# Moving the "+1" of a gate's sigmoid from ScalarE to VectorE

## The reference

```
x0 = xf @ w1 + b1;  x1 = xf @ w2 + b2;  x2 = xf @ w3 + b3      # [b, n], n = 4096 pixels
sm = softmax(x0[:, :, None] * x1[:, None, :], axis=1)
feats = einsum('bn,bnm->bm', x2, sm)                            # [b, n]
return sigmoid(feats) * x
```

## Time and profile before

| | |
|---|---|
| median of three executions | 5820.21 us |
| the profiled execution's own time | 5822.9 us |
| its span, first to last instruction | 5821.0 us |
| PE busy | 5343.6 us (92%) |
| DVE busy | 4126.1 us (71%) |
| ACT busy | 4092.6 us (70%) |
| POOL busy | 1925.5 us (33%) |
| granted clock of TensorE, mean over the span | 0.948 of full |

### The profile page before, as it was taken

How to read it: one execution, slowest core, us unless ns; L and a number is a source line. 1 busy time by engine, 2 the same in 40 slices (tenths; PEclk the granted TensorE clock), 3 DMA queues, 4 the chain that set the end, 5 groups by cost and what they waited for, 6 DMA issues and landing times.

```text
span 5821.0 us, 111758 instructions
## 1 busy us (share of the span) xinstructions
PE 5343.6 (92%) x43240; PEld 2782.0 (48%) x43240; DVE 4126.1 (71%) x8699; ACT 4092.6 (70%) x6401; POOL 1925.5 (33%) x1588
## 2 busy tenths in 40 slices
PE   5789999999999999999999999999999989999976
PEld 2435536454453645446363554645445364544514
DVE  6647777777777777677777777777777777767715
ACT  1367768678686877868677786867768587786863
POOL 1224234242423424233342423424242342423302
PEclk8899999999999999999999999999999999999976
DMA  2000110102011020101102011010201102010000
GB/s 71 16 30 19 59 30 19 61 10 66 23 56 33 12 64 14 63 26 38 46 7 70 19 59 30 21 59 10 67 22 56 33 13 64 14 62 27 16 15 30
DMA packets 163165, 211.10 MB, mean 36 GB/s; under 512 B 13136, under 2 KB 146000, under 8 KB 162640
## 3 DMA queue, kind: packets, MB, share of 16 engines
q1 hardware_dynamic: 138064, 136.82, 7.3%
q0 software_dynamic: 24576, 67.14, 4.0%
HBM read 136.80 MB, written 67.11 MB: 35 GB/s over the span
## 4 chain that ended last, share of the span: by engine, by line
PE 68%; ACT 14%; DVE 9%; issue 5%; POOL 2%; DMA 1%; SPq 0%; ACTq 0%; DVEq 0%; POOLq 0%
PE PS L1036 33%; PE PS L1200 16%; PE PS L1191 6%; ACT n_x L478 2%; PE PS L1295 2%; PE PS L1065 2%; PE PS L1087 2%; PE PS L1134 2%; ACT big L552 1%; DVE stats L753 1%; ACT work L516 1%; ACT work L515 1%; ACT xin L478 1%; ACT attn L524 1%; ACT attn L530 1%
## 5 line engine op out<-in xcount | busy, mean ns | idle before, releaser
L552 ACT ACTIVATE big<-PS 128x1024 f32<-128x1024 f32 x1376 | 1365.9, 1024 | 482.9 <-PE PS L1191 409.6
L552 ACT ACTIVATE soft<-PS 128x1024 f32<-128x1024 f32 x672 | 676.5, 1024 | 370.3 <-PE PS L1191 356.1
L391 POOL DMA_INDIRECT quant_H<-emb_t,idx x512 | 487.4, 952 | 990.4 <-DVE idx L777 806.6
L1036 PE MATMUL PS<-e_hi,n_hi 128*128 128x512 f16 x2048 | 783.3, 382 | 21.8 <-DVE m L771 13.4
L1036 PE MATMUL PS<-e_lo,n_hi 128*128 128x512 f16 x2048 | 780.1, 381 | 0.0
L1036 PE MATMUL PS<-e_hi,n_lo 128*128 128x512 f16 x2048 | 779.7, 381 | 0.0
L1200 PE MATMUL PS<-big,w 128*4 128x512 f32 x5504 | 770.0, 649 | 2.2 <-ACT big L552 2.2
L753 DVE BATCH_NORM_STATS2 stats<-XT 128x6 f32<-128x512 f32 x1024 | 651.7, 683 | 21.1 <-POOL XT L407 11.3
L1191 PE MATMUL PS<-rhs,lhs 12*128 12x512 bf16 x4096 | 565.5, 401 | 75.5 <-ACT big L552 47.1
L777 DVE FIND_INDEX8 idx<-m,work 128x8 uint32<-128x1024 f32 x512 | 622.1, 1219 | 0.0
L771 DVE CUSTOM_DVE_ANT_0 work<-PS,e_bias,m 128x512 f32<-128x512 f32 x512 | 384.1, 750 | 220.8 <-PE PS L1036 215.4
(11 more groups left out here) (216 smaller groups left out, 11128.0 us busy)
## 6 DMA issues: line engine op xcount, KB each, us to landing
xin<-x SPq DMA_DIRECT2D x128, 512.0 KB, 3.8
out<-yout SPq DMA_DIRECT2D x128, 512.0 KB, 2.9
quant_H<-emb_t,idx POOLq DMA_INDIRECT x512, 2.7
XT<-emb SPq DMA_DIRECT2D x1, 1024.0 KB, 5.0
XT<-wh SPq DMA_DIRECT2D x1, 256.0 KB, 5.0
XT<-wqv SPq DMA_DIRECT2D x1, 256.0 KB, 5.2
XT<-wk SPq DMA_DIRECT2D x1, 128.0 KB, 5.2
w_sb<-w SPq DMA_DIRECT2D x1, 128.0 KB, 5.1
```

The source lines that it names most:

```text
L391: nc.gpsimd.indirect_dma_start(quant[:, g % 2, u, :], None, emb_t, bass.IndirectOffsetOnAxis(ap=idx[:, t % (2 * GT), 0:1], axis=0),).then_ ...
L552: nc.scalar.activation(E[h % 3][:, z * 1024:(z + 1) * 1024], bank(2 * z, 2), ACT.Exp).then_inc(exped.sem, 1)
L1036: ins = mm(dst, a, b, start=first and j == 0, stop=last and j == 2)
```

## The change

ACT's "+1" is removed, with its semaphore `gate_oned`. DVE now waits for `gate_exped` (raised by the exponential), adds 1 itself with a `tensor_scalar` of 128x32 with an immediate, SBUF to SBUF and in place, and then takes the reciprocal behind a `link`.

```diff
             def gate_exp(im):
                 act.wait_ge(*gate_arg.after(im))
                 nc.scalar.activation(gate[:, 1, :], gate[:, 0, :], ACT.Exp, scale=-1.0).then_inc(gate_exped.sem, 1)
-                act.wait_ge(*gate_exped.after(im))
-                nc.scalar.activation(gate[:, 1, :], gate[:, 1, :], copy, bias=ones[:, 0:1]).then_inc(gate_oned.sem, 1)
...
                 last.then_inc(gate_arg.sem, 1)
-                dve.wait_ge(*gate_oned.after(im))
+                dve.wait_ge(*gate_exped.after(im))
+                link(v.tensor_scalar(gate[:, 1, :], gate[:, 1, :], 1.0, None, ALU.add))
                 v.reciprocal(gate[:, 2, :], gate[:, 1, :]).then_inc(gate_made.sem, 1)
```

More of the change, by code:

```diff
@@ L249, in build @@
         filled, exped, summed = step("filled", 2 * HALVES), step("exped", 2 * HALVES, 2), step("summed", HALVES, 3)
-        acc_kept, acc_turned, gate_arg, gate_exped, gate_oned, gate_made = (
-            step(n, 1) for n in ("acc_kept", "acc_turned", "gate_arg", "gate_exped", "gate_oned", "gate_made"))
+        acc_kept, acc_turned, gate_arg, gate_exped, gate_made = (
+            step(n, 1) for n in ("acc_kept", "acc_turned", "gate_arg", "gate_exped", "gate_made"))
         g_normed, g_spread = step("g_normed"), step("g_spread")
```

## The result

The changed kernel takes 5866.5 us (median of four executions, 5862.9 to 5876.9); the kernel before took 5819.8 us beside it (5818.3 to 5822.9). The ratio is 1.0083 with a 95% interval of 1.0065 to 1.01: 46.7 us slower. The forecast was 5848 us with 5815 to 5860, so the sign is right and the size is too small: the time lies 6.5 us above the range. The profiled execution of after took 5868.4 us (span 5866.5, mean granted clock 0.942 in place of 0.948).

The account below looks back on a forecast made before the run. ACT was taken to bound the touched stretch up to 890.87, PE having some room. Six images at 0.92 us plus nine at 2.6, less 0.2, gave about +28 on 5820.2: 5848 us, range 5815 to 5860.

Parts of the forecast that it names:

- The addition by itself: On DVE, between exponential and reciprocal: the 32-element addition, undisturbed, was estimated at 0.17 us.
- Held by POOL: At DVE's addition: POOL's subtraction L401 starts first and blocks it until its end, making the reciprocal 1.82 us later.
- ACT's part: On ACT at the gate: dropping the "+1" frees 0.23 us an image, 3.7 us over sixteen.
- Queueing: From the spread to ACT's L515: PE idle time absorbs 0.90 of 1.82 us, so ACT is 0.92 us late per image.
- The clock's price: Behind PE's new idle time before the spread: matmuls at the lower clock cost 1.7 us more, making 2.6 us an image.
- Nine images out of fifteen: Behind PE's new idle time: the clock was taken to fall in nine images of fifteen, bounds none and all.
- What ACT is late there goes through rigidly to 890.87 and on: From ACT's L515 onward: ACT has no idle time to absorb its lateness, so +0.92 us per image passes on.
- Not held: Rival at DVE's addition: POOL does not block it, giving a small gain, 5816.5 us; chance 0.22.
- off the path: Rival behind the gate: the engines' room absorbs the whole 1.82 us, total effect between -3.7 and +5 us; chance 0.08.
- Held, but PE keeps its clock: Rival behind the spread: POOL blocks the addition but PE's clock never falls, +14 us, 5834 us; chance 0.15.

Follow-up runs that it names:

- psum_sum: The changed kernel, with DVE's addition written to PSUM and the reciprocal reading it there; 5820.5 us, ratio 1.0.
- pool_after_gate: The changed kernel, with POOL's second layer-1 subtraction (L401) made to wait for the gate of the image before, addition left in SBUF; 5823.1 us, ratio 1.0002.
- both_ops: The kernel before, ACT's "+1" kept, with a DVE multiplication by 1.0 added between it and the reciprocal; 5867.7 us, ratio 1.0084.
- pe_filled: The changed kernel, with 16 matmuls of unused result in PE's new idle time ahead of the spread; 5823.6 us, ratio 1.0001.
- before_fill2: The kernel before, with 17 matmuls of unused result in PE's 1.96 us idle time ahead of l1_scores(new, 2); 5830.5 us, ratio 1.0011.
- psum_fill2: The changed kernel with the addition written to PSUM, plus 17 matmuls of unused result ahead of l1_scores(new, 2); 5826.6 us, ratio 1.0006.
- exp_first_b: The changed kernel, with ACT's gate exponential placed ahead of n_hi (L508), which releases POOL's subtraction; 5819.3 us, ratio 0.999.
- pad22: The kernel before, with 22 matmuls of unused result ahead of the last block of sums, where PE has no gap; 5878.1 us, ratio 1.0098.

## Why the prediction was right in its sign and too small in its size

**The addition by itself:** 0.17 us forecast, 0.181 measured. Right.

**Held by POOL:** right, and shown from three sides (psum_sum, pool_after_gate, both_ops). POOL came first by 0.01 us in all fifteen images; the reciprocal moved by 1.83 us against 1.82 forecast, and PE's idle time was 1.96 (median of the fifteen) against 1.95. The inference from the pace of the 512-element rows and from L883 carried. L883 reads two tensors, though, so it could show the hold and not that a one-source addition is open to it; psum_sum showed that. The Trainium skill's rule (SBUF — State Buffer, Who interferes with whom) and its case of an fp32 tensor_scalar from SBUF to SBUF (VectorE: DVE Perf Modes, Mode 2×_2P), which no row of before showed, are borne out: 2.15 us with SBUF as destination, 0.194 us with PSUM, beside the same POOL instruction.

**ACT's part:** 0.23 us forecast, 0.35 measured. The "+1" had waited for the exponential and so started 0.24 us after it; `gated`, which waits for nothing new, follows it in 0.12. The step counted one start distance where two are replaced by one shorter one. In psum_sum this gain shows in the stretch and not in the time.

**Queueing:** 0.92 us forecast, 0.75 measured (pe_filled), a fifth less. The clock's price: 1.7 us forecast, 1.66 measured (2.41 - 0.75). Both mechanisms hold.

**"Nine images out of fifteen": failed.** The clock fell behind the new idle time in 13. The guess came from the idle place in itself shifting between images; that place's own record was in the trace of before, where the second idle time, of the same length, is followed by slow matmuls in 14 of 15. Counting it would have given 14 for 9. With 13 of them the sum is 2 x 0.75 + 13 x 2.41 = 32.8 us, which is what the stretch shows (32).

**"What ACT is late there goes through rigidly to 890.87 and on": failed behind 890.87.** Up to there it holds: ACT's next L515, 18.37 us after the exponential before and 20.79 now, is late by the same 2.4 us. But 32 us in the stretch became 46.7, and the other 15 were in no part of the sum; that alone put the time above the range, since 5819.8 + 32.8 = 5852.6 lies inside it. The sum took the turns as a chain that passes on what it is given. They are no such chain: 2.4 to 2.5 us in the stretch came out as 3 to 4 us in eight of the fifteen turns, and gains of 0.3, 0.92 and 1.3 us an image came out as nothing (psum_sum, before_fill2, psum_fill2).

The traces show a part of what does it: the clock falls at other places. In five images of the changed kernel it falls once more, 54 to 55 us behind the exponential, where it does so in no image of before. Here is the third image, now and before, and then ACT's cast into o_hi (L584 before, L582 now), before and now:

```profile
1278.40:1281.80 3.40, 3.40 (x18) 3.40 (x17) 1.07 (x3) 3.25 (x7) 0.71 (x1) 0.50 0.00 0
...
1270.10:1273.50 3.40, 3.08 (x36) 2.70 (x31) 2.41 (x4) 3.23 (x6) 1.50 (x1) 1.00 0.02 5
```

```profile
1313.20 1.06 ACT L584 ACTIVATE o_hi<-o_x 128x1024 f16<-128x1024 f32 x1
...
1325.57 1.06 ACT L582 ACTIVATE o_hi<-o_x 128x1024 f16<-128x1024 f32 x1
```

The exponentials start at 1215.44 and 1223.74, so this cast is 4.07 us late (101.83 against 97.76), where ACT had been 2.42 us late at 50 us. In all five images the delay at 100 us is 4.0 to 4.4 us; in the other eight with slow matmuls behind the spread it is still 2.0 to 2.7. psum_fill2 shows the same with the other sign. In eleven of its fourteen long turns the clock falls 51 us behind the exponential (the second image, and the same place of before, where it is at full speed):

```profile
922.50:925.90 3.40, 3.40 (x17) 3.37 (x16) 1.07 (x3) 3.25 (x7) 0.71 (x1) 0.51 0.00 0
...
922.20:925.60 3.40, 3.40 (x48) 3.08 (x44) 1.56 (x6) 3.27 (x8) 0.71 (x1) 1.00 0.02 5
```

In ten of these eleven the 1.3 us gained at 50 us have shrunk to 0.1 or turned into a loss of up to 0.6 at 100 us. Over the whole span TensorE spends 676 us at the lower level after the change and 609 before; 68 us more at half speed are 34 us of work lost, of which 13 x 1.66 = 22 us lie behind the spread and 12 elsewhere, about the missing 11 us of the turns. In the five images the traces show such a fall and the delay that comes with it; that the further falls make up the whole of the 11 us is argued, and no run isolates why the clock falls where it does.

**The rivals.** "Not held" and "off the path" are ruled out by the 2.15 us and by L515's wait. "Held, but PE keeps its clock" was forecast at 5834; pe_filled comes nearest to that case, and took 5823.6, as the clock kept its level at the second place too.

## What to carry to other kernels

Before a small SBUF-to-SBUF `tensor_scalar` goes to VectorE, look in the trace at what GpSimd runs at that moment; if it runs a two-tensor SBUF instruction, write the result to PSUM, or move one of the two out of the other's way. Price a new wait on TensorE twice, for the time in the queue and for the lower clock behind it, and read from an idle time of like length in all its occurrences how often the clock falls. In a kernel of long equal turns, compare the lengths of the turns before adding small local gains: here gains up to 1.3 us a turn vanished and a loss of 2.4 us mostly came out as 3 to 4.

## What the runs showed of the hardware that was not expected

- A lead of 0.01 us was enough for POOL's instruction to hold the addition for 1.97 us, in all fifteen images that had both. With the addition 1.06 us ahead it is not held (exp_first_b); no run has it ahead by a hundredth.
- Sixteen matmuls that compute nothing of use, put into a wait of 2.0 us, gave back 43 us of 46.7 (5823.6 against 5866.5), without the gate coming any earlier.
- The lengths of the turns gather near 344.8, 348 and 352 us in most kernels of this study, though nothing in the code has such a step. In before, the ten turns near 344.8 have 20.5 us each at the lower clock level, the four longer ones 23.9 or 27.3; but pad22 has turns near 348 with 20.5. The cause of the steps is open, as is that of pad22's 54.6 us (median) for 43 us of matmuls.
- A clock fall that was filled away at one place came back 31 us later in most turns (psum_fill2), and took the gain with it.
- The order of two instructions can matter more than their number: with the exponential ahead of n_hi, the moved addition costs nothing (5819.3), and behind it 46.7 us.
